# Value pages on every fourth partition, keys in the same order, and the seam's store waits moved to ScalarE

## The reference, cut to what matters

```
q, k, v = x @ Wq.T, x @ Wk.T, x @ Wv.T        # 32 query heads, 8 key heads, D = 128
q, k = rope(rmsnorm(q)), rope(rmsnorm(k))
kc = k_cache[block_table]                     # 16 pages of 32 keys for each sequence: L = 512
vc = v_cache[block_table]
k_all, v_all = concat(kc, k), concat(vc, v)   # 512 + 32 = 544 keys
scores = where(valid, q . k_all * SCALE, -1e30)
o = softmax(scores) @ v_all                   # 4 query heads share one key head
x = x + o @ Wo.T
```

## Time and profile before

| quantity | value |
|---|---|
| median of 3 runs | 1297.55 us |
| the profiled execution | 1303.05 us, span 1301.2 us, mean granted clock 0.972 |
| PE busy | 1196.2 us, 92% |
| DVE, ACT, POOL busy | 849.6, 678.4, 730.6 us |
| HBM traffic | 235.74 MB read, 46.27 MB written |

### The profile page before, as it was taken

How to read it: one execution, slowest core, us unless ns; L and a number is a source line. 1 busy time by engine, 2 the same in 40 slices (tenths; PEclk the granted TensorE clock), 3 DMA queues, 4 the chain that set the end, 5 groups by cost and what they waited for, 6 DMA issues and landing times. The chain is left out here.

```text
span 1301.2 us, 28268 instructions
## 1 busy us (share of the span) xinstructions
PE 1196.2 (92%) x8010; PEld 1045.7 (80%) x8010; DVE 849.6 (65%) x1748; ACT 678.4 (52%) x1581; POOL 730.6 (56%) x567
## 2 busy tenths in 40 slices
PE   7987899999999879999999999999999974899888
PEld 5634788888888779999899899999989863787676
DVE  7585577777776757778787778777777753423323
ACT  4173344444443657777777767777767753311111
POOL 2201799999998745555555555555555522344332
PEclk9998999999999989999999999999999997899899
DMA  9265544434445699999999999999999928666562
GB/s 345 95 224 166 168 134 133 128 91 133 133 119 153 181 265 276 280 299 286 287 284 284 280 290 276 290 292 285 276 280 268 287 75 297 182 206 195 166 193 85
DMA packets 282544, 282.60 MB, mean 217 GB/s; under 512 B 56037, under 2 KB 241381, under 8 KB 282502
## 3 DMA queue, kind: packets, MB, share of 16 engines
q1 hardware_dynamic: 273430, 257.44, 68.5%
q10 hardware_dynamic: 9072, 24.65, 6.5%
HBM read 235.74 MB, written 46.27 MB: 217 GB/s over the span
## 5 line engine op out<-in xcount | busy, mean ns | idle before, releaser
L1254 ACT ACTIVATE att_prob<-att_neg,att_nmax 128x544 f32<-128x544 f32 x256 | 191.4, 748 | 152.3 <-DVE att_nmax L1074 150.6
L915 POOL TENSOR_TENSOR att_k_lo<-all_room_a,att_k_hi 128x544 fp32r<-128x544 f32 x124 | 172.3, 1391 | 140.4 <-ACT att_k_hi L1277 139.6
L1074 DVE CUSTOM_DVE_ANT_1 att_neg<-att_mask,pa_pair 128x576 f32<-128x576 f32 x256 | 192.2, 751 | 84.6 <-PE pa_pair L109 78.6
L915 POOL TENSOR_TENSOR att_k_lo<-att_kT,att_k_hi 128x544 fp32r<-128x544 f32 x128 | 174.7, 1365 | 128.0 <-ACT att_k_hi L1277 127.7
L1126 DVE COPY att_pT<-pa_pt 128x512 f32<-128x512 f32 x256 | 175.7, 686 | 23.6 <-PE pa_pt L945 23.5
L107 PE MATMUL pa_pair<-prj_wt_hi,early_xT_lo 128*128 128x512 f32 (+1 forms) x512 | 180.0, 352 | 6.5 <-DVE prj_wt_lo L1136 6.5
L108 PE MATMUL pa_pair<-prj_wt_lo,early_xT_hi 128*128 128x512 f32 (+1 forms) x512 | 174.3, 340 | 0.0
L109 PE MATMUL pa_pair<-prj_wt_hi,early_xT_hi 128*128 128x512 f32 (+1 forms) x512 | 172.7, 337 | 0.0
L107 PE MATMUL pa_pair<-att_k_hi,att_q_lo 128*128 128x288 f32 (+1 forms) x512 | 169.2, 330 | 1.0 <-POOL att_k_lo L915 1.0
L1485 POOL TENSOR_TENSOR out_o_n<-out_o_n,all_room_b 128x1024 f32<-128x1024 f32 x32 | 78.4, 2449 | 155.7 <-DMA all_room_b<-inv_scratch 155.7
L945 PE MATMUL pa_pt<-all_ident,att_prob 128*128 128x128 f32 x1024 | 154.4, 273 | 1.5 <-ACT att_prob L1254 1.5
(11 more groups left out here) (146 smaller groups left out, 2714.9 us busy)
## 6 DMA issues: line engine op xcount, KB each, us to landing
all_room_a<-in_k_cache_t SPq DMA_DIRECT2D x256, 128.0 KB, 4.1
att_kT<-in_k_cache_t SPq DMA_DIRECT2D x256, 128.0 KB, 3.9
all_room_b<-in_L_cond_v_cache SPq DMA_DIRECT2D x166, 128.0 KB, 3.7
att_vc<-in_L_cond_v_cache SPq DMA_DIRECT2D x160, 128.0 KB, 3.6
q_scratch<-prj_qst SPq DMA_DIRECT2D x64, 256.0 KB
o_scratch<-att_ost SPq DMA_DIRECT2D x32, 512.0 KB, 5.1
out_o_n<-o_scratch SPq DMA_DIRECT2D x32, 512.0 KB, 3.6
all_room_b<-inv_scratch SPq DMA_DIRECT2D x32, 512.0 KB, 6.2
```

The lines of the kernel that those rows point to most:

```text
L915: g.tensor_tensor(k_lo[j % SPLITS][:], kT[j // HK % 2][:, :, j % HK, :], f32(k_hi[j % SPLITS][:]), ALU.subtract).then_inc(k_split, 1)
L1074: v.tensor_tensor_reduce(halves[0], halves[1], ps[j % 2][:, :, 0:KA], 1.0, 3.0e38, ALU.add, ALU.min, nmax[j % 2][:]).then_inc(maxed, 1)
L1254: act.activation(prob[j // GROUP % 2][:, j % GROUP, :], neg[j % 2][:, 0:KEYS], ACT.Exp, bias=nmax[j % 2][:, 0:1], scale=-1.0, accum_out=to ...
```

## The change

Four things are edited.

1. load_value_page writes the 32 rows of page j to partitions j%4, j%4+4, ... of chunk j//4. Key r of that page then stands at partition 4*r + j%4. So that scores and mask have the same order, k_hi and k_lo become plain [128, 544] tiles whose first 512 columns are written in the order (chunk, row, page in chunk), read from kT with a step of one page (1 KB) from element to element in runs of four; the 32 new keys are a second instruction. This holds for ACT's k_hi, POOL's k_lo and DVE's k_lo of the first four units. The iota that numbers the keys gets the same pattern.
2. kq_in is divided into q_in (one DMA) and k_in (17 DMAs). DVE's q_hi waits for q_in alone, ACT's k_hi for k_in.
3. SP no longer waits for its stores in each projection unit. There are two stored semaphores, for even and odd units; ACT waits for them itself at the two places where it waited for stage_free, for the same unit's stores. SP waits for some of the stores before it loads the new keys of batches 0 and 1 (both now behind unit 57), and for all of them once, behind the loop.
4. The ten value pages of batch 1 are issued ahead of unit 62's stores, not behind them, and the two Wo loads go from the seam to a place just ahead of the last pair of batches.

```diff
 def load_value_page(eng, inp, tile, j, page, sem):
-    r = slice(j % PPT * PS, (j % PPT + 1) * PS)
-    eng.dma_start(tile[r, j // PPT, :], v_pages[bass.ds(page, 1)].rearrange("a s c -> (a s) c")).then_inc(sem, 16)
+    eng.dma_start(tile[j % PPT::PPT, j // PPT, :], v_pages[bass.ds(page, 1)].rearrange("a s c -> (a s) c")).then_inc(sem, 16)
...
-        k_hi = [after_w0.sb(f"k_hi{i}", [P, PG, PS], F32R) for i in range(SPLITS)]
+        k_hi = [after_w0.sb(f"k_hi{i}", [P, KEYS], F32R) for i in range(SPLITS)]
...
+        STORES, STORED_AT_FIRST = 3 * 16, 16
+        def units_stored(it, j):
+            return (it * (P_UNROLL // 2) + j // 2) * STORES + STORED_AT_FIRST
+        def by_row(tile):
+            return tile[:, 0:L].rearrange("p (c t m) -> p c t m", c=NCH, m=PPT)
+        def cached_pages(j):
+            return kT[j // HK % 2][:, 0:NPP, j % HK, :].rearrange("p (c m) t -> p c t m", c=NCH)
...
                     last_head = tail and slot == 1
+                    if last_head and t == TT - 2:
+                        sp.wait_ge(mm_done, UNITS)
+                        for i in range(NPP - ACT_PAGES):
+                            load_value_page(sp, inp, vc[1], i, pages1[i], v_in[1])
...
-                    sp.wait_ge(stored, (n + 1) * 48)
-                    sp.sem_inc(stage_free, 1)
-                    if last_head and t in (0, 1):
-                        load_new(sp, t, t)
-                    if last_head and t == TT - 2:
-                        sp.wait_ge(mm_done, UNITS)
-                        for i in range(NPP - ACT_PAGES):
-                            load_value_page(sp, inp, vc[1], i, pages1[i], v_in[1])
+                    if last_head and t == 1:
+                        sp.wait_ge(stored[0], units_stored(it, TT + 2))
+                        load_new(sp, 0, 0)
+                        load_new(sp, 1, 1)
...
-                for i in range(2):
-                    load_wo(sp, inp, i, wo[i], wo_in[i])
+                for s in range(2):
+                    sp.wait_ge(stored[s], UNITS // 2 * STORES + STORED_AT_FIRST)
...
                 with sp.Fori(0, B // 2 - 1) as it:
                     batches(it, False)
+                for i in range(2):
+                    load_wo(sp, inp, i, wo[i], wo_in[i])
                 batches(B // 2 - 1, True)
...
-                g.iota(key_no[:, 0:L], pattern=[[1, L]], base=0, channel_multiplier=0,
+                g.iota(key_no[:, 0:L], pattern=[[P, NCH], [1, PS], [PS, PPT]], base=0, channel_multiplier=0,
...
-                    g.tensor_tensor(k_lo[j % SPLITS][:], kT[j // HK % 2][:, :, j % HK, :], f32(k_hi[j % SPLITS][:]),
+                    g.tensor_tensor(by_row(k_lo[j % SPLITS]), cached_pages(j), f32(by_row(k_hi[j % SPLITS])), ALU.subtract)
+                    g.tensor_tensor(k_lo[j % SPLITS][:, L:KEYS], kT[j // HK % 2][:, NPP, j % HK, :], f32(k_hi[j % SPLITS][:, L:KEYS]),
...
-                        dve.wait_ge(kq_in[g * GROUP // HK % 2], (it + g * GROUP // UNROLL + 1) * 16 * (PG + 1))
+                        dve.wait_ge(q_in[g * GROUP // HK % 2], (it + g * GROUP // UNROLL + 1) * 16)
...
-                        act.wait_ge(kq_in[j // HK % 2], (it + j // UNROLL + 1) * 16 * (PG + 1))
-                    act.activation(k_hi[j % SPLITS][:], kT[j // HK % 2][:, :, j % HK, :], ACT.Copy).then_inc(k_hi_done, 1)
+                        act.wait_ge(k_in[j // HK % 2], (it + j // UNROLL + 1) * 16 * PG)
+                    act.activation(by_row(k_hi[j % SPLITS]), cached_pages(j), ACT.Copy)
+                    act.activation(k_hi[j % SPLITS][:, L:KEYS], kT[j // HK % 2][:, NPP, j % HK, :], ACT.Copy).then_inc(k_hi_done, 1)
...
-                        act.wait_ge(stage_free, n - 1)
+                        act.wait_ge(stored[j % 2], v_read(it, j))
...
-                    act.wait_ge(stage_free, n + 1)
+                    act.wait_ge(stored[j % 2], units_stored(it, j))
```

More of the change, by code:

```diff
@@ L669, in stage_project_attend @@
         after_w0 = Region(nc, "att", at_w0, WT)
-        k_hi = [after_w0.sb(f"k_hi{i}", [P, PG, PS], F32R) for i in range(SPLITS)]
-        k_lo = [after_w0.sb(f"k_lo{i}", [P, PG, PS], F32R) for i in range(SPLITS)]
+        k_hi = [after_w0.sb(f"k_hi{i}", [P, KEYS], F32R) for i in range(SPLITS)]
+        k_lo = [after_w0.sb(f"k_lo{i}", [P, KEYS], F32R) for i in range(SPLITS)]
         pnT = [after_w0.sb(f"pnT{i}", [P, GROUP, P]) for i in range(2)]
@@ L710, in stage_project_attend @@
         q_staged = m.sem("q_staged")
-        stage_free = m.sem("stage_free")
         ids_in = m.sem("ids_in")
-        stored = m.sem("stored")
+        stored = [m.sem(f"stored{i}") for i in range(2)]
         lens_ready = m.sem("lens_ready")
-        kq_in = [m.sem(f"kq_in{i}") for i in range(2)]
+        k_in = [m.sem(f"k_in{i}") for i in range(2)]
+        q_in = [m.sem(f"q_in{i}") for i in range(2)]
         v_in = [m.sem(f"v_in{i}") for i in range(2)]
@@ L776, in load_keys @@
         def load_keys(eng, b, slot, pages):
-            load_new_keys(eng, q_d, k_d, b, q[slot], kT[slot], kq_in[slot])
+            load_new_keys(eng, q_d, k_d, b, q[slot], kT[slot], q_in[slot], k_in[slot])
             for j, page in enumerate(pages):
-                load_key_page(eng, inp, kT[slot], j, page, kq_in[slot])
+                load_key_page(eng, inp, kT[slot], j, page, k_in[slot])
         def load_new_values(eng, b, slot):
@@ L801, in _ @@
             def _(sp):
-                sp.sem_inc(stage_free, 2)
+                for s in range(2):
+                    sp.sem_inc(stored[s], STORED_AT_FIRST)
                 load_head(sp, inp, 1, wn[1][:], w_in[1])
@@ L936, in scores @@
                         pe.wait_ge(k_split, n + 1)
-                    three_pass(pe, ps[i][:, 0, 0:KA], qh, ql, k_hi[x][:, 0:PA, :], k_lo[x][:, 0:PA, :], True, True)
-                    three_pass(pe, ps[i][:, 1, 0:KB], qh, ql, k_hi[x][:, PA:PG, :], k_lo[x][:, PA:PG, :],
+                    three_pass(pe, ps[i][:, 0, 0:KA], qh, ql, k_hi[x][:, 0:KA], k_lo[x][:, 0:KA], True, True)
+                    three_pass(pe, ps[i][:, 1, 0:KB], qh, ql, k_hi[x][:, KA:KEYS], k_lo[x][:, KA:KEYS],
                                True, True).then_inc(scored, 1)
@@ L1130, in split_k_lo @@
                     dve.wait_ge(k_hi_done, n + 1)
-                    v.tensor_tensor(k_lo[n][:], kT[0][:, :, n, :], f32(k_hi[n][:]), ALU.subtract).then_inc(k_split_first, 1)
+                    v.tensor_tensor(by_row(k_lo[n]), cached_pages(n), f32(by_row(k_hi[n])), ALU.subtract)
+                    v.tensor_tensor(k_lo[n][:, L:KEYS], kT[0][:, NPP, n, :], f32(k_hi[n][:, L:KEYS]), ALU.subtract).then_inc(k_split_first, 1)
                 def split_lo(k, slot, done):
```

24 lines of the change are left out of this document (13 added, 11 removed).

## The result

The changed kernel took 1321.8 us in the median, beside 1294.0 us of the kernel before in the same comparison; the ratio is **1.022**, 95% interval 1.012 to 1.033. The forecast of 1277 us was wrong by 45 us and in sign. One execution with every product of TensorE about 1.6 times as long stood among the first four (2431.9 us, and it was the profiled one): the median of the other three is 1317.6 us, and the profile after is read from x1_after, profiled at 1319.25 us, span 1317.4 (before: 1303.05 and 1301.2).

The account below looks back on a forecast made before the run. It took attention as PE-bound, with 30.4 us lost to late loads through SP's full queue. Terms -8.3 (seam), -15 (q_in, k_in), +2.5 (first units) sum to -20.8 us, giving 1277 us on the median's scale; range 1264 to 1306.

Parts of the forecast that it names:

- Value pages: Value-page loads to every fourth partition: as many issues as before, nothing beside the other gain, bounds -7 and +5 us.
- R1: Rival: value pages move faster, SP's pages are not held up, PE is the bound; 1267 us, chance 0.12.
- k_hi on ACT: ACT's k_hi, 256 times: second instruction 0.2 us, step 0 to 0.1, upper bound 0.40; ACT 2.0 to 2.1 a unit.
- R2: Rival: the step costs ACT its upper bound, 2.38 us a unit; 1285 to 1292, say 1288 us, chance 0.20.
- k_lo on POOL: POOL's k_lo, 252 times: 1.58 to 2.22 us, taken 1.8, hidden within a unit of 2.32 us.
- R4: Rival: POOL becomes the bound at L915 in each unit, slower; middle 1335 us, chance 0.15.
- First units: Four k_hi, four k_lo and the longer group unit on ACT lengthen some steps: +2.5 us, bounds 0 and 6.
- Seam: Value pages ahead of unit 62's stores and Wo moved away, so q of batch 2 goes earlier: gain 8.3 us, bounds 5 and 9.
- q_in, k_in: DVE's stalls before q_hi go, ACT awaits key pages one unit later: gain 15 us, 13.4 to 18.7.
- SP's unbroken pace: SP's queue at 18.89 us a batch is the next bound, 0.31 above dense, 8.7 us over 28 batches.
- R3: Rival: only the seam gains; SP's queue holds 19.3 us a batch whoever waits for it; 1289 us, chance 0.15.
- Wo late: Wo's 7.3 us of transfer is covered by the last two batches, over 35 us; no cost counted.

Follow-up runs that it names:

- x1_after: The changed kernel itself, unedited, measured and profiled a second time: 1318.4 us, 1.027 of the kernel before.
- x5: The changed kernel with ACT's k_hi back to one plain instruction in page order, value pages still on every fourth partition: 1320.7 us, 1.023.
- x8: The changed kernel with value pages on neighbouring partitions and ACT's k_hi plain, only k_lo and mask in the new order: 1271.2 us, 0.987.
- x14: The changed kernel without part 1, SP reading its ten value-page numbers a second time each batch: 1297.6 us, 1.010.
- x13: The changed kernel with plain k_hi on ACT, strided value pages, and eight instead of six value pages issued by ACT: 1282.4 us, 0.988.
- x7: The changed kernel with value pages back on 32 neighbouring partitions, ACT's stepped k_hi kept: 1294.1 us, 1.003.
- x16: The changed kernel with part 1 undone, parts 2 to 4 kept, measured again in five rounds: 1271.0 us, 0.990.
- x11: The kernel before with parts 3 and 4 of the change alone: 1278.0 us, 0.990.
- x10: The kernel before with part 2 alone, q's arrival on its own semaphore: 1279.8 us, 0.988.
- x15: The changed kernel without part 1, each value page on 8 partitions with four rows each, PE turning probabilities with a four-column step: 1699.0 us, 1.307.

## Why the prediction was wrong

*Value pages, the failed step.* The text says "SP and ACT issue as many as before" and gives it nothing, bounds -7 and +5. The number of issues was right and their duration was never priced. SP's queue had just been named as the next bound, above PE's pace already. Ten issues at +172 ns are 1.7 us a batch, 50 us in 29 batches; of that the pages alone cost 44.2 us by the pace (x5 over x8), 1.5 us a batch. ACT's step added 0.2 us a batch on top of them (x1_after 20.96, x5 20.74). The row for this sum, the same instruction with another pattern, was not in the trace of before, so its cost was to be bounded and put into the range, as was done for ACT's step. What was read as a possible relief, faster landing, did come: the median landing of value pages on SP's queue fell from 3.6 to 2.9 us, of key pages from about 4 to 2.8, and the share from 1.00 to 0.85. Part of that is only the slower loop: in x14, with near pages, key pages landed in 2.6 to 3.0 us too. But x13 keeps it at nearly the old rate (282 GB/s at a share of 0.90, key pages 2.7, value pages 3.2). It is worth nothing while SP's issue sets the pace. So R1 saw the transfers rightly and its "against" (the issue alone is 18.89 us) was the sentence to follow to its end.

*k_hi on ACT.* The second instruction cost 0.21, as taken. The step was taken at 0 to 0.1 us, with 0.40 as its upper bound; it cost 0.50, over the bound. The reduce of DVE that gave the bound was no proxy for ACT. R2 had the mechanism and a price too low: x7 is its pure case, at 1294.1 us, or 21 us over x8 by the pace where the rival allowed 11. It stayed hidden behind SP's pace in the changed kernel.

*k_lo on POOL.* 1.8 taken, 1.92 measured, hidden; R4 was out. The step cost 0.24 us for 512 columns over the 1.32 of the prediction's line, inside its 0 to 0.40.

*First units.* +2.5 taken. PE waits 2.0 us for the first k_lo of POOL in the changed kernel, and its busy time in 438 to 443 is 3.22 us where x16 has 4.37. Right in size.

*Seam.* 8.3 taken, 13.2 measured in x11 (1 to 25 by its interval), the hole of 6 us gone. SP's first q load comes 7.1 us earlier. Right in kind, and near in size where the trace shows it.

*q_in, k_in.* 15 taken, 15.2 measured in x10. Right in kind; that the number agrees so closely is luck, since its interval runs from 3 to 27 us, and the last q load of x10 is 11.9 us earlier. Both terms were added to 23.3, and the kernels with both gained 13 to 21.

*SP's unbroken pace.* 18.89 us was taken from one step of the queue. In x16 SP waits 0.5 us in 500 and its pace is still 19.35, with ACT waiting 27.6 us for key pages: what R3 said of the queue (19.3 whoever waits). R3's sum of 8.3 was still too small a gain. The prediction also put the 3.1 us between output store and q down to register loads; the load of 16 numbers (L576) takes 2.17 us in the median.

*Wo late.* ACT waits 2.6 us for it in the output part of x16, 1.8 before. Nothing, as said.

*The range.* Its upper end, 1306, was set by the cheap end of the POOL rival. No case put two queues over the limit, though the forecast's own words ("late next is SP's own pace") asked for one.

## What to carry to other kernels

Where a queue of DMA issues is full, the price of an issue is part of every change to a transfer's shape: read the issue's own duration by line, multiply by its count a period, and compare with the slack of that queue before thinking of bandwidth. When a change loads two resources near the limit, undo one at a time and both: a single repair may show nothing (x5) although what it repairs is over the limit too (x7). And a dose on the suspected resource alone (x14: 1 us of queue time a batch, 27 us in the end) tells a pace-setter from a bystander.

## What the runs showed of the hardware

- Issuing 32 rows of 4 KB to partitions with a step of four took 543 ns on SP and 480 on ACT, to 32 neighbouring ones 371 and 322; 8 partitions with four rows each took 277 and 515. In x14, whose page numbers come from a second reading, the neighbouring form took 316.
- ACT's copy of 512 columns took 1110 ns with a read step of 1 KB and 1143 with a write step of 16 bytes, where 0.83 ns an element (0.43 us, plus 0.19 fixed) is its rate in runs of 32. POOL's subtraction of 512 columns in the same order took 1.56 us, where 544 plain ones took 1.39: about 0.24 us more, as an estimate by the 2.2 ns an element of the prediction's line.
- PE's weight loads from probabilities with a step of 16 bytes (x15, L953) took 211 ns, where they took 140 without it (x16). The other large groups of loads were 11 to 19% longer in x15, whose mean granted clock was 0.83; its unstepped loads of L959 took 140.
- With value pages on every fourth partition the DMA engines moved 265 GB/s at a share of 0.85 (x1_after, 500 to 1000 us: 312 at a full share) and 282 at 0.90 (x13: 313). With near pages they moved 284 at 1.01 before, and 272 at 0.93 (292) in x14, which is slower as well. The bytes do travel better; nothing waited for them.
